# One-hots of the destinations made stationary in the attribute sums, the first layer's own share moved into the build, and another order at the build's end

## The chip, the core and the metric

The kernel is one program on one core of a Trainium2 chip. The metric is device microseconds of one execution. Five engines of the core run their own instruction streams and meet at semaphores: PE (TensorE, matrix products into the eight PSUM banks), DVE (VectorE), ACT (ScalarE), POOL (GpSimd) and SP (SyncE, which here only starts DMAs).

## The reference

Five message-passing layers on 3125 nodes and 53125 edges, then a mixture of experts. Only the graph part matters here.

```python
norm = dinv[row] * dinv[col]
h = x                                          # layer norm of the input
for l in range(5):
    edge_fea = concat([edge_attr[:, 3:] @ ew1[l], edge_attr[:, 0:3] @ ew2[l]])
    msg = norm[:, None] * (h[row] + edge_fea)
    agg = segment_sum(msg, col, num_segments=n)
    h = relu(concat([h, agg], axis=1) @ mlp_w[l] + mlp_b[l])
    h = (h - mean(h)) * rsqrt(var(h) + eps) * bn_g[l] + bn_b[l]
    if l != 4: h = relu(h)
```

The product with `mlp_w` splits in two: `h @ mlp_w[:256]`, the nodes' **own share**, and `agg @ mlp_w[256:]`. The own share of layer 0 needs nothing of the edges. The edge attributes reach `agg` only through the sum of each destination's four scaled attributes, the **attribute sums**; these are the same in all layers.

## The kernel before

All features are kept transposed: `hT` and `aggT` have 128 partitions (channels of one half h of two) and 3125 columns (nodes). The columns go in NQ = 7 groups `COLS`, six of 500 and one of 125.

**The build.** The adjacency matrix is made on the chip as counts, 25 source tiles of 125 rows by 3125 destinations (`at`). The edges, sorted by destination, are taken in 63 windows w of 50 destinations; with these inputs each window is one turn of 8 chunks of 128 edges. For a turn DVE makes three one-hot tiles (L1575 to L1582: `ohS` of the source's place, `ohD` of the destination, `cnt1`), double-buffered by `side` = w % 2, and raises `s_oh`. PE then does 8 matmuls for the attribute sums (L1817: `now`, 12 columns of attribute parts, is the stationary operand and `ohD`, 50 columns, moves) and 8 for the counts (L1819). Two windows make a pair u. After a pair PE closes the bank (L1823, `s_cnt`), ACT copies it (L1671, `s_enc`), DVE splits it in nibbles (L1545, L1549, `s_nib`) and ACT writes five pieces of `at` with sums (L1689, `s_at`). DVE does the nibbles of pair u after the window 2u + 3.

Between the windows PE has more work, in the order of its program: two transposes a window of the input's tiles (`across`, L1736; four banks, ACT copies each to `hT` at L1644 in `turned`), and **dense units**. A unit is one source tile of one group g = (column group, half): two matmuls of up to 500 columns with `m` stationary (L699). Layer 0's aggregation is 14 groups g of 25 units, 350 units in all. `dense_after(w)` says how many are done by window w: at most six a window, from window 13 on, and 50 in each ten windows, so that one window in ten (w = 22, 32, ...) has none. A group ends with its attributes (L705, which wait for `s_s4Te`), and DVE evicts it (L724).

**The attribute sums' way.** The sums of a block b of ten windows stand as 12 rows by 500 columns in bank 2 or 3. ACT copies them out (`sums_out`, L1659), PE transposes them by four tiles of 125 (`turn_sums`, L1772, in window 10b + 12), DVE adds and splits them in three bf16 parts (`attribute_sums`, L1561 to L1565), PE turns these back into rows (`turn_rows`, L1778), ACT writes them to `s4T` (`rows_out`, L1664).

**The build's end.** After window 62 PE has 100 units left (groups 10 to 13). Its order: `turn_sums(5)` in the loop, `turn_rows(5)`, 25 units, `turn_sums(6)`, 25 units, `turn_rows(6)`, a check sum, the last 50 units of 125 columns. DVE's order: the nibbles of pairs 30 and 31 (the latter wait for ACT), then both `attribute_sums`, then the evictions of groups 8 on. A group g >= 3 starts only when group g - 3 is evicted.

**The linear step** (`linear_pe`, L786): for each column group PE multiplies `wcur` with `hT` (own share) and with `aggT`, in f32, 16 matmul records a group, 8 of them own share. ACT adds the bias and takes the relu from PSUM (L886); DVE takes statistics (L846), at the end their aggregate (L849). The same code serves all layers. After it PE runs 14 matmuls on zeros (L746) until the next layer's transposes (L680).

Of the kernel before, what the change touches and what calls it, by code (L numbers as in the profile page):

```python
# [82 lines left out]
def gnn_ffn_program(nc, x, src, dst, edge_attr, mlp_w, mlp_b, ew1, ew2, bn_g, bn_b,  # L83
                    wg, bg, gbias, w1, b1, w2, b2, out):
    ctx = ExitStack()
    with ctx:
# [46 lines left out]
        r.at = max(r.at, w_at + 12288)  # L133
# [10 lines left out]
        eps = r("eps", [128, 1], F32)  # L144
# [20 lines left out]
        s4r = r("s4r", [12, CQ], F32)  # L165
# [21 lines left out]
        s4h = r("s4h", [P, BT, PARTS, PARTS, 4], BF16)  # L187
        assert r.at <= w_end
        cnt1 = []
# [138 lines left out]
        s4P = r("s4P", [P, BT, 4], F32)  # L328
# [54 lines left out]
        s_s4r = sem("s_s4r")  # L383
        s_s4t = sem("s_s4t")
# [21 lines left out]
        s_hd = sem("s_hd")  # L406
        s_ls = sem("s_ls")
# [73 lines left out]
        EWB = bank[7]  # L481

        def sums_of(b):

            return bank[2 + b % 2][0:12, 0:min(CQ, NW * W - CQ * b)]

        def tiles_of(b):

            return range(BT * b, min(BT * (b + 1), NT))
# [287 lines left out]
        def linear_pe(pe, base, following):  # L777
            pe.wait_ge(s_wc, base(1) + 1)
            for q, (a, w) in enumerate(COLS):
                pe.wait_ge(s_agge, base(H * NQ) + H * (q + 1))  # L780
                if q >= 2:
                    pe.wait_ge(s_z, base(ZC) + H * (q - 1))
                for k in range(2 * H):
                    rhs = (hT if k < H else aggT)[:, k % H, a:a + w]
                    for h in range(H):
                        last = pe.matmul(bank[2 * (q % 2) + h][:, 0:w], wcur[:, k, h * 128:(h + 1) * 128], rhs, start=k == 0, stop=k == 2 * H - 1)  # L786
                        if k == 2 * H - 1:
                            last.then_inc(s_mlp, 1)
# [22 lines left out]
        def statistics_dve(dve, base, following):  # L811
# [10 lines left out]
            if not last_layer:  # L822
# [12 lines left out]
                attribute_parts(dve, step, lambda: dve.tensor_tensor(ewS[:, :, :], ewT[:, :, :], cfi[:, 1, :].bitcast(F32).unsqueeze(2).to_broadcast([128, H, 4]), ALU.mult))  # L835
            for q, (a, w) in enumerate(COLS):
                if q == NQ - 1:
                    dve.wait_ge(s_mlp, base(H * NQ) + H * NQ)
                    step(dve.tensor_scalar(hT[:, 1, a:a + w], bank[2 * (q % 2) + 1][:, 0:w], prm[:, 0, 1:2], 0.0, ALU.add, ALU.max))
# [42 lines left out]
        def linear_act(act, base, following):  # L882
            for q, (a, w) in enumerate(COLS):
                for h in range(H if q < NQ - 1 else 1):
                    act.wait_ge(s_mlp, base(H * NQ) + H * q + h + 1)
                    act.activation(hT[:, h, a:a + w], bank[2 * (q % 2) + h][:, 0:w], ACT.Relu, bias=prm[:, 0, h:h + 1]).then_inc(s_z, 1)  # L886
# [359 lines left out]
        def _(sp):  # L1246
# [35 lines left out]

            sp.wait_ge(s_cnt, PAIRS)
# [53 lines left out]
        def _(dve):  # L1337
# [213 lines left out]
            def attribute_sums(b):  # L1551

                tiles = tiles_of(b)
                n = len(tiles)
                x, parts = s4P[:, 0:n, :], s4h[:, 0:n, :, :, :]

                def thrice(v):
                    return v.unsqueeze(2).to_broadcast([P, n, PARTS, 4])

                dve.wait_ge(s_s4t, b + 1)  # L1560
                step(dve.tensor_reduce(x, TURN[0:P, 0:12 * n].rearrange("p (t k j) -> p t j k", t=n, k=3), axis=XYZ, op=ALU.add))  # L1561
# [50 lines left out]
            with dve.If(gathers == 0):  # L1612
                for l in range(L):
                    if l:
                        aggregate_dve(dve, layer(l), LOADS * (l + 1))
                    statistics_dve(dve, layer(l), layer(l + 1) if l + 1 < L else None)
            with dve.If(gathers == 1):
                gather_dve(dve, 0)
                statistics_dve(dve, layer(0), layer(1))
# [9 lines left out]
        def _(act):  # L1629
# [12 lines left out]
            def turned(t):  # L1642
                act.wait_ge(s_xT, t + 1)
                act.activation(hT[:, :, t * P:(t + 1) * P], bank[4 + t % 4][:, 0:H * P].rearrange("p (h n) -> p h n", h=H), ACT.Copy).then_inc(s_xTe, 1)  # L1644
# [9 lines left out]

            def sums_out(b):
# [229 lines left out]
```

## Time and profile before

| | us |
|---|---|
| Median of three runs | 1605.82 (1603.84 to 1607.27) |
| The profiled execution | 1611.95 |
| its span, first to last instruction | 1610.3 |
| PE busy | 1421.4 |
| DVE busy | 674.2 |
| ACT busy | 399.4 |

The profile's page gives busy time of the engines and the chain of work that ended last. The timeline gives start and duration in microseconds; a line "x8" is eight instructions from the start of the first to the end of the last. A square bracket at its end is idle time of that engine ahead of it and who ended it. Matmul records overlap, so that the spacing of two starts, not the duration of one, is what a matmul costs in a stream. PEclk is the granted clock of TensorE, where 1.00 is 2.4 GHz and 0.50 is 1.2 GHz.

### The profile page before, as it was taken

What the parts mean: (1) busy time and instruction counts of PE and PEld (TensorE: products, weight loads), DVE (VectorE), ACT (ScalarE), POOL (GpSimd) and SP (SyncE); (2) the same over time, 40 slices, a digit from 0 to 9 for tenths busy, and PEclk for the clock granted to TensorE, in tenths of its full rate; (3) what the DMA queues carried; (4) which work ended last, traced back from release to release, by engine and by line L of the source; (5) the groups of instructions that cost most, each with busy time, mean ns of one, the idle gap of its engine ahead of it and who ended that gap; (6) DMA issues with size and microseconds to landing.
All of it is one profiled execution on the core that took longest, in us unless ns stands there. A gap on an engine that the chain in (4) does not pass through costs nothing.

```text
span 1610.3 us, 25262 instructions
## 1 busy us (share of the span) xinstructions
PE 1421.4 (88%) x9032; PEld 851.9 (53%) x9033; DVE 674.2 (42%) x1562; ACT 399.4 (25%) x1032; POOL 175.5 (11%) x147
## 2 busy tenths in 40 slices
PE   2566589999899999999999999999999873899996
PEld 2555344444444544545445554445445442899995
DVE  7989888887622310122101320023100267333442
ACT  1320354444402400033001420014100240244442
POOL 2000000000000000000000000000000003477774
PEclk9876789999989999999999999999999976999998
DMA  5144000000000000000000000000001383244443
GB/s 124 56 157 161 1 1 2 1 2 1 15 1 0 14 0 1 1 14 0 1 0 1 14 1 0 1 0 15 0 1 46 62 276 96 42 70 69 71 71 44
DMA packets 49545, 57.76 MB, mean 36 GB/s; under 512 B 14320, under 2 KB 41602, under 8 KB 49185
## 3 DMA queue, kind: packets, MB, share of 16 engines
q1 hardware_dynamic: 38688, 41.67, 9.0%
q0 software_dynamic: 10752, 14.69, 5.5%
q8 instruction: 67, 1.10, 0.3%
q14 instruction: 38, 0.30, 0.1%
HBM read 42.36 MB, written 13.99 MB: 35 GB/s over the span
## 4 chain that ended last, share of the span: by engine, by line
PE 80%; DVE 12%; issue 4%; DVEq 2%; ACT 1%; DMA 1%; POOL 1%; SPq 0%; POOLq 0%
PE bank L690 33%; PE bank L786 13%; PE bank L699 10%; PE bank L1214 6%; PE bank L1223 6%; PE bank L1819 3%; DVE ohL L1467 1%; PE bank L680 1%; PE bank L1760 1%; PE bank L705 1%; PE bank L1817 1%; PE bank L1205 1%; PE bank L1180 1%; DVEq L512 1%; PE bank L1742 1%
## 5 line engine op out<-in xcount | busy, mean ns | idle before, releaser
L690 PE MATMUL bank<-at,m 125*128 125x500 fp8e4 (+1 forms) x2800 | 550.9, 351 | 3.5 <-DVE m L647 3.5
L690 PEld LDWEIGHTS bank<-at,m 125*128 125x128 f16 x2800 | 252.4, 97 | 259.8 <-issue 7.1
L724 DVE TENSOR_TENSOR aggT<-bank,dinvB 128x500 f32<-128x500 f32 (+1 forms) x70 | 42.3, 622 | 389.0 <-PE bank L690 355.8
L886 ACT ACTIVATE hT<-bank,prm 128x500 f32<-128x500 f32 (+1 forms) x65 | 42.5, 654 | 569.2 <-PE bank L786 569.2
L699 PE MATMUL bank<-at,m 125*128 125x500 fp8e4 (+1 forms) x700 | 155.4, 376 | 6.8 <-issue 2.5
L935 POOL TENSOR_TENSOR idJ<-idJ,wts 125x1400 f32<-125x1400 f32 x2 | 8.0, 4006 | 1346.0 <-DVE idJ L1093 1346.0
L1214 PEld LDWEIGHTS bank<-xtT,w1c 128*128 128x128 f32 x896 | 111.2, 196 | 2.8
L1214 PE MATMUL bank<-xtT,w1c 128*128 128x128 f32 x896 | 111.4, 279 | 0.0
L786 PE MATMUL bank<-hT,wcur 128*128 128x500 f32 (+1 forms) x280 | 111.1, 539 | 0.0
L786 PE MATMUL bank<-aggT,wcur 128*128 128x500 f32 (+1 forms) x280 | 110.8, 538 | 0.0
L699 PEld LDWEIGHTS bank<-at,m 125*128 125x128 f16 x700 | 63.5, 103 | 83.6 <-issue 33.5
L1223 PE MATMUL bank<-w2s,h1T 128*128 x448 | 106.1, 380 | 0.0
L846 DVE BATCH_NORM_STATS2 zst<-hT 128x6 f32<-128x500 f32 x60 | 40.9, 681 | 153.2 <-ACT hT L886 153.2
L647 DVE SCALAR_TENSOR_TENSOR m<-bank,dinvP,m 125x256 f16<-125x256 f32 x100 | 47.3, 483 | 132.6 <-ACT m L669 132.6
L951 POOL DMA_INDIRECT out_rows<-ytb,rowS x56 | 95.7, 1709 | 53.1 <-issue 23.5
L1689 ACT ACTIVATE at<-encB 125x500 fp8e4<-125x500 uint8 (+1 forms) x96 | 57.5, 599 | 120.7 <-DVE encB L1545 118.1
L1223 PEld LDWEIGHTS bank<-w2s,h1T 128*128 128x128 f32 x448 | 80.8, 190 | 9.2 <-issue 0.2
L786 PEld LDWEIGHTS bank<-aggT,wcur 128*128 128x128 f32 x280 | 50.4, 190 | 55.1 <-issue 55.1
L786 PEld LDWEIGHTS bank<-hT,wcur 128*128 128x128 f32 x280 | 50.1, 190 | 53.4 <-issue 53.2
L1580 DVE TENSOR_TENSOR cnt<-iotaK,nowKD 128x2000 bf16<-128x2000 int16 x63 | 75.2, 1194 | 0.0
L1819 PE MATMUL bank<-cnt,ohS 128*128 128x250 bf16 x504 | 74.3, 293 | 0.0
L1000 ACT ACTIVATE h1T<-bank,b1T 128x128 f32<-128x128 f32 x224 | 64.0, 368 | 25.4 <-issue 20.5
(318 smaller groups left out, 1413.8 us busy)
## 6 DMA issues: line engine op xcount, KB each, us to landing
slrow<-sl_dram SPq DMA_DIRECT2D x26, 512.0 KB, 4.8
w1s<-in_L_ffn_W SPq DMA_DIRECT2D x1, 4096.0 KB, 13.8
w2s<-in_L_ffn_W SPq DMA_DIRECT2D x1, 4096.0 KB, 20.5
xin<-in_x SPq DMA_DIRECT2D x1, 2800.0 KB
x<-in_x SPq DMA_DIRECT2D x1, 2800.0 KB
out_rows<-x SPq DMA_DIRECT2D x1, 2800.0 KB
xn_dram<-xn SPq DMA_DIRECT2D x1, 2800.0 KB
wraw<-in_L_gnn_mlp_w SPq DMA_DIRECT2D x5, 512.0 KB, 3.5
```

The source lines that it names most:

```text
L647: dve.scalar_tensor_tensor(m[:, t, 1, :], bank[t % 4][0:P, 0:D], dinvP[:, t:t + 1], m[:, t, 0, :], ALU.mult, ALU.subtract).then_inc(s_lo, 1)
L690: last = pe.matmul(bank[LATER[g % len(LATER)]][:, 0:w], m[:, s, k, h * 128:(h + 1) * 128], at_block(g // H)[:, s, :], start=False, stop=s ...
L699: pe.matmul(bank[FIRST[g % len(FIRST)]][:, 0:w], m[:, s, k, h * 128:(h + 1) * 128], at_block(g // H)[:, s, :], start=s == 0 and k == 0, st ...
L786: last = pe.matmul(bank[2 * (q % 2) + h][:, 0:w], wcur[:, k, h * 128:(h + 1) * 128], rhs, start=k == 0, stop=k == 2 * H - 1)
L886: act.activation(hT[:, h, a:a + w], bank[2 * (q % 2) + h][:, 0:w], ACT.Relu, bias=prm[:, 0, h:h + 1]).then_inc(s_z, 1)
L951: pool.indirect_dma_start(out[:, :], bass.IndirectOffsetOnAxis(ap=rowS[:, j:j + 1], axis=0), ytb[:, j % XB, :], None, compute_op=ALU.add). ...
L1000: last = act.activation(h1T[:, u, k, :], bank[4 + u][:, k * TT:(k + 1) * TT], ACT.Relu, bias=b1T[:, bass.ds(e, 1), k:k + 1].rearrange("p a ...
L1214: last = pe.matmul(bank[4 + u][:, k * TT:(k + 1) * TT], w1c[:, u, h, k * 128:(k + 1) * 128], xtT[:, u, h, :], start=h == 0, stop=h == H - 1)
L1223: last = pe.matmul(bank[6 + u][:, 0:D], h1T[:, u, k, :], w2s[:, bass.ds(e, 1), k, :].rearrange("p a f -> p (a f)"), start=k == 0, stop=k = ...
L1580: dve.tensor_tensor(cnt1[side][:, :, :, :], to_all(iotaK[:, :, :], U // 2), by_pairs(nowKD[:, side, 0, :], GW), ALU.is_equal)
L1689: last = act.activation(at_block(q)[:, field:field + FIELDS * (GROUPS - 1) + 1:FIELDS, a:a + n], byte[:, f, :, 0:n], ACT.Copy, saturate=False,
L1819: last = pe.matmul(out_w, ohS[side][:, j // 2, :, j % 2], cnt1[side][:, j // 2, :, j % 2].rearrange("p (g n) -> p g n", g=GROUPS), start=F ...
```

## The change

Three things. In the attribute sums the operands change places: `ohD` is stationary (50 columns) and `now` moves (12 columns). The sums of a window stand as 50 rows by 12 columns, so that DVE reads them from PSUM without `sums_out` and `turn_sums`; `turn_rows` works with ten strips of 50 rows in place of four tiles of 125.

The own share of layer 0 is computed in the build: PE does it for column group q after window 2q + 4 (`own_share`), ACT adds the bias and writes it back into `hT`; the weights come by a DMA of their own (`w1z`). In layer 0 PE then does only the `aggT` half; DVE adds the own share (`add_own`), ACT takes the relu. Since the own share takes banks 6 and 7, `across` has two banks in place of four.

At the build's end PE takes six units before `turn_rows(5)` and 44 behind it; DVE takes `attribute_sums(5)` and the evictions of groups 8 and 9 before the nibbles of pair 31; ACT writes the rows of block 5 before its last pieces of `at`.

```diff
@@ attribute_sums (DVE)
-                dve.wait_ge(s_s4t, b + 1)
-                step(dve.tensor_reduce(x, TURN[0:P, 0:12 * n].rearrange(...), axis=XYZ, op=ALU.add))
+                dve.wait_ge(s_s4, b + 1)
+                if b:
+                    dve.wait_ge(s_s4T, b)
+                step(dve.tensor_reduce(x, sums_of(b).rearrange("p (t k j) -> p t j k", t=n, k=3), axis=XYZ, op=ALU.add))
@@ the build's end (DVE)
-            for u in range(PAIRS - 2, PAIRS):
-                low_nibbles(u)
-                high_nibbles(u)
+            low_nibbles(PAIRS - 2)
+            high_nibbles(PAIRS - 2)
             attribute_sums(NQ - 2)
+            dve.wait_ge(s_cnt, PAIRS)
+            for g in range(evicted, H * NQ - 2 * H):
+                evict(dve, zero, g, FIRST)
+            low_nibbles(PAIRS - 1)
+            high_nibbles(PAIRS - 1)
             attribute_sums(NQ - 1)
...
-            for g in range(evicted, H * NQ - H):
+            for g in range(H * NQ - 2 * H, H * NQ - H):
@@ statistics (DVE)
+            def add_own(q):
+                a, w = COLS[q]
+                for h in range(H):
+                    dve.wait_ge(s_mlp, H * q + h + 1)
+                    dve.tensor_tensor(hT[:, h, a:a + w], bank[2 * (q % 2) + h][:, 0:w], hT[:, h, a:a + w], ALU.add).then_inc(s_ad, 1)
+            if first_layer:
+                add_own(0)
             for q, (a, w) in enumerate(COLS):
+                if first_layer and q + 1 < NQ:
+                    add_own(q + 1)
@@ SP
+            sp.wait_ge(s_ds, NLB)
+            sp.dma_start(w1z[:, :, :], mlp_w[0:1, 0:D, :].rearrange("a (k p) c -> p (a k) c", p=128)).then_inc(s_wz, 16)
+                sp.dma_start(biasz[:, :], mlp_b[0:1, :].rearrange("a (h p) -> p (a h)", p=128)).then_inc(s_wz, 16)
@@ the pairs (ACT)
-                        sums_out(b)
                 for t in range(4 * u + (u > 0), min(4 * u + 5, NT)):
                     turned(t)
+                if 2 <= u < NQ + 2:
+                    a, w = COLS[u - 2]
+                    act.wait_ge(s_pz, u - 1)
+                    for h in range(H):
+                        act.activation(hT[:, h, a:a + w], OWN[h][:, 0:w], ACT.Identity, scale=2.0 ** -H0_EXP, bias=biasz[:, h:h + 1]).then_inc(s_hz, 1)
+                if u == PAIRS - 1:
+                    rows_out(NQ - 2)
@@ PE
             def across(t):
-                if t >= 4:
-                    pe.wait_ge(s_xTe, t - 3)
+                if t >= 2:
+                    pe.wait_ge(s_xTe, t - 1)
+            def own_share(q):
+                a, w = COLS[q]
+                pe.wait_ge(s_xTe, min((q + 1) * BT, NT))
+                if q == 0:
+                    pe.wait_ge(s_wz, 32)
+                    pe.wait_ge(s_ewm, 1)
+                else:
+                    pe.wait_ge(s_hz, H * q)
+                for k in range(H):
+                    for h in range(H):
+                        last = pe.matmul(OWN[h][:, 0:w], w1z[:, k, h * 128:(h + 1) * 128], hT[:, k, a:a + w], start=k == 0, stop=k == H - 1)
+                last.then_inc(s_pz, 1)
+                        if g == 1:
+                            pe.wait_ge(s_hz, H * NQ)
-                        pe.matmul(sums_w, now[:, side, 0:12, j], ohD[side][:, j // 2, :, j % 2], start=False, stop=False)
+                        pe.matmul(sums_w, ohD[side][:, j // 2, :, j % 2], now[:, side, 0:12, j], start=False, stop=False)
-                for t in range(2 * w + (w > 0), min(2 * w + 3, NT)):
+                for t in range(2 * w + (w > 1), min(2 * w + 2 + (w > 0), NT)):
                     across(t)
-                if w > SB and w % SB == 2:
-                    turn_sums(w // SB - 1)
+                if w >= 4 and w % 2 == 0 and w // 2 - 2 < NQ:
+                    own_share(w // 2 - 2)
+            done = dense_to(min(done + DENSE_W, DENSE))
             turn_rows(NQ - 2)
-            done = dense_to(min(done + NT, DENSE))
-            turn_sums(NQ - 1)
-            done = dense_to(min(done + NT, DENSE))
+            done = dense_to(min(done + 2 * NT - DENSE_W, DENSE))
             turn_rows(NQ - 1)
```

## Rows read from the trace of the kernel before

**Rows 1.** Timeline, PE in windows 3 and 4: start, us, engine, line, form, idle before.
```profile
180.73 0.36 PE L1817 MATMUL bank<-ohD,now 128*12 128x50 bf16 x8 [1.22 <-DVE ohS L1582]
...
181.94 0.16 PE L1823 MATMUL bank<-zeros 128*128 128x1 bf16 x1
...
182.82 0.38 PE L1808 MATMUL bank<-zeros 128*128 128x500 bf16 x1
...
184.67 0.36 PE L1817 MATMUL bank<-ohD,now 128*12 128x50 bf16 x8 [1.47 <-DVE ohS L1582]
```

**Rows 2.** Timeline, PE: turns of windows 13, 14, 15 and 23, window 14's units.
```profile
218.65 0.49 PE L1817 MATMUL bank<-ohD,now 128*12 128x50 bf16 x8 [1.15 <-DVE ohS L1582]
...
225.59 0.39 PE L1817 MATMUL bank<-ohD,now 128*12 128x50 bf16 x8
...
227.11 2.71 PE L699 MATMUL bank<-at,m 125*128 125x500 fp8e4 x12
...
229.75 0.39 PE L1817 MATMUL bank<-ohD,now 128*12 128x50 bf16 x8
...
263.10 0.49 PE L1817 MATMUL bank<-ohD,now 128*12 128x50 bf16 x8 [1.21 <-DVE ohS L1582]
```

**Rows 3.** Timeline, PE from the last window to the last units.
```profile
438.55 0.60 PE L1772 MATMUL bank<-ident,s4r 12*125 12x12 f32 x4
...
444.35 0.60 PE L1778 MATMUL bank<-negI,s4h 125*36 125x125 bf16 x4 [5.20 <-DVE s4h L1565]
444.88 13.29 PE L699 MATMUL bank<-at,m 125*128 125x500 fp8e4 x50
...
460.86 12.14 PE L699 MATMUL bank<-at,m 125*128 125x500 fp8e4 x50 [2.17 <-DVE aggT L724]
```

**Rows 4.** Table by stretch, linear step: us, busy time (instructions) of each engine, PEclk, DMA.
```profile
480.00:500.00 20.00, 20.00 (x49) 9.03 (x48) 5.52 (x22) 3.39 (x5) 0.00 (x0) 1.00 0.00 1
```

**Rows 5.** Timeline, layer 0's linear step: own shares of groups 0 and 5, end, next layer.
```profile
479.65 3.62 PE L786 MATMUL bank<-hT,wcur 128*128 128x500 f32 x8
...
513.29 3.52 PE L786 MATMUL bank<-hT,wcur 128*128 128x500 f32 x8
...
523.35 0.55 DVE L849 BATCH_NORM_AGGREGATE zmv<-zst 128x2 f32<-128x42 f32 x2
...
526.80 0.67 PE L680 MATMUL bank<-ident,hT 128*125 128x128 f32 x4 [0.60 <-DVE hT L644]
```

**Rows 6.** Timeline, window 1: the bank's close, ACT's copies, the transposes behind them.
```profile
175.09 0.16 PE L1823 MATMUL bank<-zeros 128*128 128x1 bf16 x1
175.32 0.59 ACT L1671 ACTIVATE encI<-bank 125x500 int32<-125x500 f32 x1 [21.18 <-PE bank L1823]
...
175.81 1.46 ACT L1644 ACTIVATE hT<-bank 128x250 f32<-128x250 f32 x5
...
176.24 0.43 PE L1736 MATMUL bank<-ident,xin 125*128 125x125 f32 x2 [0.34 <-ACT hT L1644]
```

**Rows 7.** The page's groups: busy us, mean ns, idle before and its releaser.
```profile
L724 DVE TENSOR_TENSOR aggT<-bank,dinvB 128x500 f32<-128x500 f32 (+1 forms) x70 | 42.3, 622 | 389.0 <-PE bank L690 355.8
...
L846 DVE BATCH_NORM_STATS2 zst<-hT 128x6 f32<-128x500 f32 x60 | 40.9, 681 | 153.2 <-ACT hT L886 153.2
...
L1689 ACT ACTIVATE at<-encB 125x500 fp8e4<-125x500 uint8 (+1 forms) x96 | 57.5, 599 | 120.7 <-DVE encB L1545 118.1
```

**Rows 8.** Instructions by line: ns min/median/max, first and last start, forms (PEld: weight loads).
```profile
L1817 PE MATMUL bank<-ohD,now x504: 183/186/220, 170.4 to 437.3; 128*12 128x50 bf16 x168
...
L1825 PEld LDWEIGHTS bank<-zeros x7: 84/84/84, 204.7 to 438.5; 128*12 128x12 bf16 x7
...
L1778 PEld LDWEIGHTS bank<-negI,s4h x25: 93/98/155, 231.3 to 473.2; 125*36 125x36 bf16 x25
...
L1772 PEld LDWEIGHTS bank<-ident,s4r x25: 178/183/184, 216.9 to 458.4; 12*125 12x125 f32 x25
```

**Rows 9.** Timeline, the lookups ahead of the build: 25 columns moving, 128 stationary.
```profile
150.65 1.36 PE L1760 MATMUL bank<-dpart,ohT 125*128 125x25 bf16 x48
```

More of the change, by code:

```diff
@@ L781, in linear_pe @@
                 if q >= 2:
-                    pe.wait_ge(s_z, base(ZC) + H * (q - 1))
-                for k in range(2 * H):
+                    pe.wait_ge(s_ad, H * (q - 1)) if first else pe.wait_ge(s_z, base(ZC) + H * (q - 1))
+                for k in range(first, 2 * H):
                     rhs = (hT if k < H else aggT)[:, k % H, a:a + w]
                     for h in range(H):
-                        last = pe.matmul(bank[2 * (q % 2) + h][:, 0:w], wcur[:, k, h * 128:(h + 1) * 128], rhs, start=k == 0, stop=k == 2 * H - 1)
+                        last = pe.matmul(bank[2 * (q % 2) + h][:, 0:w], wcur[:, k, h * 128:(h + 1) * 128], rhs, start=k == first, stop=k == 2 * H - 1)
                         if k == 2 * H - 1:
@@ L1692, in _ @@
                 last.then_inc(s_at, 1)
-            for b in range(NQ - 2, NQ):
-                rows_out(b)
+            rows_out(NQ - 1)
             for l in range(L):
@@ L1766, in _, with turn_rows @@
             pe.wait_ge(s_xn, NT)
-            def turn_sums(b):
-                pe.wait_ge(s_s4r, b + 1)
+            def own_share(q):
[4 more added lines that the diff above has]
+                    pe.wait_ge(s_ewm, 1)
+                else:
+                    pe.wait_ge(s_hz, H * q)
[3 more added lines that the diff above has]
+                last.then_inc(s_pz, 1)
+            def turn_rows(b):
                 pe.wait_ge(s_s4Te, b) if b else pe.wait_ge(s_xTe, NT)
-                for n, t in enumerate(tiles_of(b)):
-                    last = pe.transpose(TURN[0:P, 12 * n:12 * (n + 1)], s4r[:, n * P:(n + 1) * P], ident[0:12, 0:12])
-                last.then_inc(s_s4t, 1)
-            def turn_rows(b):
                 pe.wait_ge(s_s4K, b + 1)
-                for n, t in enumerate(tiles_of(b)):
-                    last = pe.matmul(TURN[0:K4, n * P:(n + 1) * P], s4h[:, n, :, :, :].rearrange("p a b j -> p (a b j)"), negI[0:P, 0:P], start=True, stop=True)
+                for n in range(strips_of(b)):
+                    last = pe.matmul(TURN[0:K4, n * W:(n + 1) * W], s4h[:, n, :, :, :].rearrange("p a b j -> p (a b j)"), negI[0:W, 0:W], start=True, stop=True)
                 last.then_inc(s_s4T, 1)
@@ L1810, in _ @@
                     if b >= 2:
-                        pe.wait_ge(s_s4r, b - 1)
-                    pe.matmul(sums_of(b), zeros[:, 0:12], nought(sums_of(b).shape[1]), start=True, stop=False)
+                        pe.wait_ge(s_s4K, b - 1)
+                    pe.matmul(sums_of(b), zeros[:, 0:W], nought(12 * strips_of(b)), start=True, stop=False)
                 with pe.Fori(0, mine) as i:
```

80 lines of the change are left out of this document (41 added, 39 removed).

## The prediction

> **What bounds the kernel now.** The page's busy times come first: PE works 1421 of 1610 us, so a change pays where PE waits, runs at half clock or loses work. The timeline of PE then shows four stretches that the change touches. In the early windows PE waits for DVE's one-hots: 1.22 us ahead of window 3, 1.47 ahead of window 4 [rows 1]. From window 13 on six dense units fill a window and PE is the bound: windows 14 and 15 start without a wait, 4.16 us apart [rows 2]. Window 13 itself lasts 6.94 us (218.65 to 225.59): its eight sums take 0.49 us where window 14's take 0.39, which is TensorE at 1.2 GHz in place of 2.4 after the waits before it [rows 2]. One window in ten has no units; there PE waits 1.21 us for DVE and falls to half clock again (window 23, 0.49) [rows 2]. At the build's end PE stands 5.20 us for the split of block 5's sums, and 2.17 us for an eviction [rows 3]. In layer 0's linear step PE is busy without a hole at granted clock 1.00 [rows 4]; a column group takes (513.29 - 479.65) / 5 = 6.73 us, and its own share half of it, 3.36 [rows 5].
>
> **The linear step of layer 0.** Six own shares of 500 columns leave it: 6 x 3.36 = 20.2 us off the path. The seventh, of 125 columns (about 0.9, a quarter), goes into the tail. DVE takes on two adds a group, of the eviction's form (PSUM and SBUF in, 0.62 us), beside two statistics of 0.68 [rows 7]: 2.6 us in 3.36, so PE stays the bound, though narrowly. ACT's relu, now from SBUF, hangs behind the add, not in PE's way. What is late next is the tail. Today group 5 ends at 479.65 + 6 x 6.73 = 520.0, and the aggregate of the statistics starts at 523.35, 3.3 us on [rows 5]. Afterwards DVE has, from the end of group 5, one add 0.62, group 4's statistics 1.36, two adds of 125 columns 0.6 (taken at half), group 5's statistics 1.36, a relu 0.3, two small statistics 0.7, and some 0.3 of gaps: 5.2. So the step gains 20.2 - 1.9 = **18.3 us**. Bounds: 20 if the tail hides, 15 if DVE's 2.6 became more than PE's 3.36 by a tenth or two.
>
> **The start of layer 1.** PE's idle time ahead of the next transposes is 0.60 us today [rows 5], because the 14 matmuls on zeros end just before them. PE now finishes some 1.9 us earlier against DVE, so it stands about 2.5 us. A hole of 2.17 us was followed by a slowed stretch [rows 3], priced below at 1.3. I take **+1 us**, between 0 and the 2.8 that window 13 lost.
>
> **The build's end.** A 500-column matmul in a clean stream costs (2.71 - 0.38) / 11 = 0.212 us (twelve in 2.71 [rows 2]; one record of 500 columns lasts 0.38 [rows 1]), so 50 of them 49 x 0.212 + 0.38 = 10.8. Group 10 took 13.29 and group 11 12.14 [rows 3]: 2.5 and 1.3 us of half clock behind the two holes. With six units first, `turn_rows(5)` comes 2.7 us after the last window. Its input, DVE's `attribute_sums(5)`, then waits only for the nibbles of pair 30, not for those of 31, so it is done before. Group 11 needs group 8's eviction, which DVE does at once after window 62. ACT writes block 5's rows while PE is in group 10, before it is asked for them. Behind each of the two steps that DVE moves ahead stand the nibbles of pair 31, which wait for ACT's copy anyway and are needed only 10 us later, by group 12. The gain is 5.20 + 2.17 + 2.5 + 1.3 + 0.6 (`turn_sums(5)`, four transposes [rows 3]) = 11.8, with the single transpose of block 6 **12 us**. Bounds: 4 if the first hole stays, 12.5.
>
> **The own share in the build.** PE gets 6 x 3.36 + 0.9 = 21 us more, in windows 4 to 16. What of it is hidden? The windows 4 to 13 take (218.65 - 184.67) / 4.5 = 7.55 us a pair [rows 1, 2]. After: the odd window has its turn, 1.21 (180.73 to 181.94 [rows 1]). Its transposes now have two banks and wait for ACT's copy of a tile, which stands behind the copy of the counts: 1.15 us from the bank's close to the transposes (175.09 to 176.24 [rows 6]), where 0.4 stands today. Two transposes with a copy of 0.29 (1.46 / 5 [rows 6]) between them take 0.8, the zeros for the next pair 0.3: 3.5 in all. The even window: turn 1.21, two transposes 0.65 (0.88 from the close to the zeros, less the dispatch [rows 1]), the share 3.36: 5.2. A pair takes 8.7, so +1.2, over 4.5 pairs +5.4, and +1 once in window 3, where ACT still writes pair 0's pieces when PE asks for a tile. Then share 5 in window 14 adds its 3.4, share 6 in window 16 0.9, and group 1 waits perhaps 0.5 in window 17 until ACT has emptied bank 6. Against that, PE is busy before window 13, so its 6.94 become 4.16: -2.8, since f32 matmuls hold clock 1.00 [rows 4]. Sum **+8.5 us**. Bounds: +1.5 if the five early shares fit wholly into the waits (3.4 + 0.9 - 2.8), +21 if nothing is hidden. ACT has room for the 14 new copies (about 0.6 each, 1.3 a pair): it sat 118 us waiting for nibbles over 32 pairs, 3.7 a pair [rows 7]. On SP the two new DMAs follow the lookups and are landed long before window 4; nothing queued behind them is wanted before the last window.
>
> **The sums with the one-hots stationary.** Today eight matmuls span 0.36 us and one lasts 0.186 [rows 1, 8]: (0.36 - 0.186) / 7 = 25 ns each, with 50 columns moving. The lookups, with 25 columns moving and 128 stationary, run at (1.36 - 0.19) / 47 = 25 ns too, one record taken as long [rows 9]. So 12 columns save nothing; a gain is excluded as far as that row reaches. A cost could come from loading 50 columns where 12 were. Loads of bf16 take 84 ns for 12 columns and 93 at the least for 36, 0.38 ns a column; the f32 load of 125 columns takes 183 [rows 8], 0.88 a column above the first. At 0.38, 50 columns are 19 ns and hide within the 25. At 0.88 they are 44, 19 more a matmul, 0.15 a turn, over some 45 turns where PE is the bound 6.8 us. I take the bf16 rows, of the same type and shape: **0**, bounds 0 and +7. The Trainium skill speaks against this change: TensorE: Matmul & The Clock Gate, section LDWEIGHTS (loading the stationary operand), gives a load's time as its columns divided by 1.2 (ns), and section Weight-path perf modes makes only full loads of 128 fast. By that, 50 columns are 42 ns and the sum is 6 us worse; the two bf16 rows here grow at less than half of that rate.
> The removed turns sit in the window in ten in which PE waits 1.21 us for DVE [rows 2], so they give nothing but at the end (counted). DVE's split now handles 120 elements on 50 partitions in place of 48 on 125, perhaps +0.4 us a block. It stands in the window where PE is at half clock behind DVE, so 0; without that cover 6 x 0.4 = 2.4.
>
> **Sum.** +8.5 + 0 - 12 - 18.3 + 1 = -20.8. The profiled execution took 1611.95 (span 1610.3 and 1.65 around it), which becomes 1591.2. That execution stands 6.1 above the median of the runs, so the median becomes 1605.82 - 20.8 = 1585.0.
>
> **The rivals.**
> Loads bind the sums: 50 stationary columns at 0.88 ns each, +6.8, **1592**. For it: the 125-column row and its slope. Against: the bf16 rows. This is also what the skill's rule would give, within a microsecond.
> The early shares hide wholly: +1.5 in place of +8.5, **1578**. For it: PE's waits of 1.2 to 1.5 us in each early window [rows 1]. Against: the wait for ACT between the two transposes.
> A hole stays at the end: `attribute_sums(5)` still stands behind the nibbles of pair 30, which need ACT's copy after pair 29's pieces; were those late, PE would stand again and fall to half clock. 5.2 + 2.5 given back, **1593**.
> Slower than before: TensorE stays at 1.2 GHz in windows 4 to 17, because short f32 bursts between waits don't lift it. A share then takes 6.7, all seven 42, no wait is long enough to hide them, and window 13 gains nothing. 42 - 12 - 18.3 + 1 = +12.7, **1618**. It decides from a build cost of 29 us on. For it: window 13's half clock after windows of short work. Against: the granted 1.00 of the same matmuls in the linear step, and the fuller windows.
> The build cost lands between, near 14 to 16 (two waits a pair in place of one): **1591**.
>
> **How the numbers follow.** Forecast 0.46 (1585, own range 1581 to 1589); loads 0.16; cost between 0.11; hidden wholly 0.11; hole 0.08; half clock 0.04, and 0.04 for a build that just eats the gain. 0.2% is 3.2 us, about what the runs here can tell apart. All cases but the last two are below 1602: faster 0.92, same 0.03, slower 0.05. The range reaches from the wholly hidden case to two of the costs together: 1577 to 1598.
>
> **What would show it.** Right: the distance from window 3 to 13 grows by 5 to 7 us and window 13 takes about 4.2; the eight sums still 0.36 to 0.39; no PE hole over 1 us between window 62 and the linear step, and that stretch near 29 us; the linear step from 43.7 to about 25 us, with DVE's adds ending inside PE's groups. Wrong: eight sums at 0.45 or more (loads), shares of 6.7 (clock), a wait at L1778 after window 62 (hole), or DVE adds well above 0.62, which would make DVE the bound of the step.

## The result, and the profile of the changed kernel

| | before | after |
|---|---|---|
| Median | 1605.81 (1603.84 to 1607.27, six runs) | 1588.11 (1586.53 to 1593.09, six runs) |
| Ratio | | 0.9896, 95% interval 0.9879 to 0.9912 |
| Profiled execution | 1611.95 | 1591.14 |
| its span | 1610.3 | 1589.4 |

The changed kernel is 17.7 us faster; 20.8 were forecast. To see where, both spans are cut at the same points of the program: the starts of the counts of windows 3, 13 and 62, of the linear step's first matmul, of the statistics' aggregate and of the 13th record of layer 1's transposes. Both kernels were later profiled once more, unchanged ("again"); those columns become important below.

| stretch, us | before | after | before again | after again |
|---|---|---|---|---|
| start to window 3 | 181.0 | 182.7 | 181.3 | 181.3 |
| windows 3 to 13 | 38.1 | 43.4 | 38.1 | 43.4 |
| windows 13 to 62 | 218.4 | 218.8 | 213.5 | 217.8 |
| window 62 to the linear step | 42.2 | 30.0 | 40.2 | 30.0 |
| linear step to the aggregate | 43.7 | 24.7 | 43.7 | 24.7 |
| aggregate to layer 1's 13th transpose | 12.6 | 15.6 | 12.6 | 14.3 |
| the rest | 1074.3 | 1074.1 | 1074.7 | 1073.9 |

**Early windows.** Timeline of PE in the changed kernel, from the close of one pair through the next (columns as in [rows 1]):

```profile
183.79 0.16 PE L1859 MATMUL bank<-zeros 128*128 128x1 bf16 x1
184.93 0.71 PE L1763 MATMUL bank<-ident,xin 125*128 125x125 f32 x4 [0.98 <-ACT hT L1676]
...
185.78 0.39 PE L1853 MATMUL bank<-now,ohD 128*50 128x12 bf16 x8
...
187.80 3.52 PE L1805 MATMUL bank<-hT,w1z 128*128 128x500 f32 x8
191.25 0.39 PE L1853 MATMUL bank<-now,ohD 128*50 128x12 bf16 x8
...
194.48 0.39 PE L1853 MATMUL bank<-now,ohD 128*50 128x12 bf16 x8
```

The wait for one-hots [rows 1] is gone, but PE stands 0.98 us ahead of an odd window's transposes. With two banks they wait until ACT has copied a tile that the even window transposed, and ACT copies the pair's counts first. The share takes 3.5 us at full clock. The next such waits end at 193.63 and 202.41, so a pair takes 8.7 to 8.8 us, where it took 7.55.

**The end.** Timeline of PE from the last window's turn; it answers to [rows 3]:

```profile
446.08 2.71 PE L704 MATMUL bank<-at,m 125*128 125x500 fp8e4 x12
448.72 0.42 PE L1812 MATMUL bank<-negI,s4h 50*36 50x50 bf16 x10
449.07 8.21 PE L704 MATMUL bank<-at,m 125*128 125x500 fp8e4 x38
...
457.53 10.75 PE L704 MATMUL bank<-at,m 125*128 125x500 fp8e4 x50
...
474.95 20.39 PE L791 MATMUL bank<-aggT,wcur 128*128 128x500 f32 x48
```

There is no hole of PE up to the linear step. Group 10 takes 2.71 + 8.21 and group 11 10.75, where they took 13.29 and 12.14 behind holes of 5.20 and 2.17.

**The linear step.** Timeline of DVE in it; the bracket is DVE's idle time and who ended it:

```profile
484.48 0.68 DVE L845 TENSOR_TENSOR hT<-bank,hT 128x500 f32<-128x500 f32 x1 [0.67 <-PE bank L791]
485.31 0.68 DVE L845 TENSOR_TENSOR hT<-bank,hT 128x500 f32<-128x500 f32 x1 [0.16 <-PE bank L791]
485.91 1.25 DVE L865 BATCH_NORM_STATS2 zst<-hT 128x6 f32<-128x500 f32 x2
...
499.69 0.55 DVE L868 BATCH_NORM_AGGREGATE zmv<-zst 128x2 f32<-128x42 f32 x2
```

DVE waits for PE in each group (0.67 + 0.16 us of 3.36), so PE is still the bound. [rows 5]'s aggregate came 43.7 us after the step's start; now it comes 24.7 after.

**The start of layer 1.** Timeline of PE ahead of and behind the next transposes:

```profile
497.98 3.16 PE L751 MATMUL bank<-zeros 128*128 128x500 bf16 x14
503.14 0.67 PE L685 MATMUL bank<-ident,hT 128*125 128x128 f32 x4 [2.00 <-DVE hT L649]
504.68 3.52 PE L695 MATMUL bank<-at,m 125*128 125x500 fp8e4 x8 [0.87 <-DVE m L652]
```

The matmuls on zeros now end 2.00 us before they are relieved (0.60 in [rows 5]), and the eight matmuls behind take 3.52 us; at full clock they take 1.86 (below).

### The profile page after: what moved, and what is told of

It is laid out like the page before. It is cut to its first block, busy times and chain, and to the rows that moved or that the text cites. A ratio compares the mean times of both kernels' runs of the same rounds, so it can differ in the third digit from the quotient of the medians.

```text
span 1589.4 us, 25320 instructions
## 1 busy us (share of the span) xinstructions
PE 1408.4 (89%) x9045; PEld 846.1 (53%) x9046; DVE 681.6 (43%) x1576; ACT 403.7 (25%) x1039; POOL 174.9 (11%) x147
## 4 chain that ended last, share of the span: by engine, by line
PE 81%; DVE 11%; issue 3%; ACT 1%; DVEq 1%; DMA 1%; POOL 1%; SPq 0%; POOLq 0%
PE bank L695 34%; PE bank L791 12%; PE bank L704 9%; PE bank L1237 6%; PE bank L1246 6%; PE bank L1855 3%; PE bank L1787 2%; DVE ohL L1494 2%; PE bank L685 1%; PE bank L1805 1%; PE bank L1853 1%; PE bank L710 1%; PE bank L1228 1%; PE bank L1203 1%; PE bank L1181 1%
## 5 line engine op out<-in xcount | busy, mean ns | idle before, releaser
L909 ACT ACTIVATE hT<-bank,prm 128x500 f32<-128x500 f32 (+1 forms) x52 | 34.0, 654 | 529.5 <-PE bank L791 529.5
L865 DVE BATCH_NORM_STATS2 zst<-hT 128x6 f32<-128x500 f32 x60 | 40.2, 679 | 123.6 <-ACT hT L909 123.6
L791 PE MATMUL bank<-hT,wcur 128*128 128x500 f32 (+1 forms) x224 | 88.8, 539 | 0.0
L674 ACT ACTIVATE m<-bank,dinvP 125x256 f16<-125x256 f32 x100 | 46.1, 473 | 98.0 <-PE bank L685 97.2
## 6 DMA issues: line engine op xcount, KB each, us to landing
w2s<-in_L_ffn_W SPq DMA_DIRECT2D x1, 4096.0 KB, 20.9
```

Source lines behind the costliest of these rows:

```text
L674: act.activation(m[:, t, 0, :], bank[t % 4][0:P, 0:D], ACT.Copy, scale=dinvP[:, t:t + 1]).then_inc(s_hi, 1)
```

## The experiments

**Both kernels once more, unchanged.** In the first profile of before, the five windows that follow a window without units or an idle stretch (13, 23, 33, 43, 53) lasted 6.8 us each from counts to counts, mostly at 1.2 GHz (granted clock 0.56).

> The kernel before, unchanged, profiled once more. In the profile that the prediction rests on, windows 13, 23, 33, 43 and 53 each run wholly at half clock (6.8 us from turn to turn), while three changed kernels show 5.5 to 6.3 there. Theory (how far the clock falls in those windows differs from execution to execution, and the first profile caught a long one, 6 us above the median): here these windows last 5.4 to 6.3 us, window 62 starts 3 to 6 us earlier than 437.1, and the time is 1603 to 1608. Rival (the kernel before always falls that far, the turned sums cure it): 6.8 us again, and the profile's surplus lies elsewhere.

> The changed kernel, unchanged, on the chip of the other runs of this call: the base for them. Both theories: 1586 to 1591 and a ratio of 0.987 to 0.991.

Measured: before 1605.83 us, span 1604.1; after 1589.10 (1587.13 to 1591.10), ratio 0.9894 [0.9878, 0.9911], span 1585.4. The five windows of before now take 5.50, 6.02, 6.39, 5.45 and 5.71 us. Timeline of PE in window 23 of that profile; [rows 2] has it in the other:

```profile
262.04 0.37 PE L1817 MATMUL bank<-ohD,now 128*12 128x50 bf16 x8 [1.21 <-DVE ohS L1582]
...
263.68 4.22 PE L699 MATMUL bank<-at,m 125*128 125x500 fp8e4 x12 [0.26 <-issue]
```

Behind the same wait of 1.21 us the eight sums take 0.37 us here and 0.49 there, and only the units are slow, 4.22 in place of 2.71. So the clock falls later, or for less time, behind the same idle stretch: how much it costs differs from execution to execution. The first profile had the expensive end of it, all five times, and was 6.2 us longer. Between the two second profiles the change is -18.7 us: build to window 62 +9.6, end -10.2, linear step -18.95, start of layer 1 +1.7, the rest -0.8. Between the two first ones it is -20.9: +7.5, -12.2, -18.95, +3.0, -0.2.

**One part at a time.** The theory is that the three parts add, with the prices of the prediction.

Sums alone, with the split and `turn_rows` that go with them and without `sums_out` and `turn_sums`; own share and order of the end as before.

```diff
-                        pe.matmul(sums_w, now[:, side, 0:12, j], ohD[side][:, j // 2, :, j % 2], start=False, stop=False)
+                        pe.matmul(sums_w, ohD[side][:, j // 2, :, j % 2], now[:, side, 0:12, j], start=False, stop=False)
...
```

> Only the turned attribute sums: own share in the linear step and the old order at the end. Theory (a stream of 8 small matmuls runs at 25 to 27 ns each in both forms, and the removed turns stood beside a wait for DVE): within 2 us of the kernel before, 1604 to 1607, window 62 within 1 us of 437.1. Rival A (loads of 50 columns bind): 6 us slower than before. Rival B (the removed turns and copies are worth something in every ten windows): 3 to 6 us faster than before.

Measured: 1604.39 us, ratio 0.9996 [0.9986, 1.0006]. From window 22 to 62 it takes 173.9 us, before again 174.1: operands in either place cost the same. At the end PE stands 5.98 us for the split, but the 2.17 us wait for an eviction is gone: 37.8 us from window 62 to the linear step against 40.2.

Sums and order, own share left in the linear step, `across` with its four banks again:

```diff
-                if w >= 4 and w % 2 == 0 and w // 2 - 2 < NQ:
-                    own_share(w // 2 - 2)
...
-                    linear_pe(pe, layer(l), layer(l + 1) if l + 1 < L else None, 0 if l else H)
+                    linear_pe(pe, layer(l), layer(l + 1) if l + 1 < L else None)
...
```

> The changed kernel with the own share back in layer 0's linear step (16 records a group, no add on DVE, transposes on four banks as before). Theory: window 62 starts 7.5 us earlier, at about 437; the linear step is 19 us longer; layer 1 starts at full clock again, 3 us gained: 8.5 us slower than the changed kernel, about 1596 to 1597. Rival (the 7.5 us of the build are due to the turned sums, as slower weight loads would make them): window 62 stays at 443 or later and the kernel is 16 us slower, 1604.

Measured: 1596.55 us (1594.75 to 1598.52), ratio 0.9952 [0.9935, 0.9968]. The linear step begins 30.0 us after window 62, 7.8 earlier than with the sums alone, and the two medians differ by 7.8: that is the order's worth. Window 62 comes at 432.8 us, where before again has 432.9 and after again 442.5; so the whole +9.7 in the build is the own share, with the two banks that it leaves to `across`. Against it stand -18.95 in the linear step and +1.7 behind it: -7.5 in the traces, and 7 to 9 less in the runs (1589.10 against 1596.55, of two chips; 0.9894 against 0.9952 of before).

The changed kernel with the old order at its end, on DVE and ACT too:

```diff
-            done = dense_to(min(done + DENSE_W, DENSE))
             turn_rows(NQ - 2)
-            done = dense_to(min(done + 2 * NT - DENSE_W, DENSE))
+            done = dense_to(min(done + NT, DENSE))
+            done = dense_to(min(done + NT, DENSE))
             turn_rows(NQ - 1)
...
```

> The changed kernel with the old order at the build's end (PE: turn_rows(5) ahead of the units; DVE: both nibbles, both attribute_sums, then the evictions; ACT: rows of block 5 last). Theory (each part gives what the sum of steps says): the holes of 5.2 and 2.2 us and the half clock behind them come back, 12 us lost against the changed kernel (1588 to about 1600); everything up to window 62 stays. Rival (the holes belong to the old sums' way and are mostly gone with turn_sums, or the later end of the windows has let ACT and DVE catch up): 3 to 6 us lost, a hole of under 3 us at turn_rows(5).

Measured: 1598.73 us (1593.14 to 1602.10), ratio 0.9956 [0.9939, 0.9973]. Timeline of PE behind the last window:

```profile
454.57 0.57 PE L1807 MATMUL bank<-negI,s4h 50*36 50x50 bf16 x10 [5.98 <-DVE s4h L1593]
455.07 13.14 PE L704 MATMUL bank<-at,m 125*128 125x500 fp8e4 x50
...
468.45 10.75 PE L704 MATMUL bank<-at,m 125*128 125x500 fp8e4 x50
```

The hole is back, and behind it group 10 loses 13.14 - 10.75 = 2.4 us at half clock: 8.4 us together, of the 10 by which the medians differ. Put in last, the order is thus worth some 10 us, and put on top of the sums alone 7.8; this kernel's runs spread over 9 us, so the parts add within what can be told apart. The wait for an eviction doesn't come back. It was missing with the sums alone too, so the order didn't remove it. Timeline of DVE at the end of the kernel before:

```profile
458.72 0.17 DVE L1561 TENSOR_REDUCE s4P<-bank 125x4 f32<-125x12 f32 x1 [14.43 <-PE bank L1772]
...
460.05 1.84 DVE L724 TENSOR_TENSOR aggT<-bank,dinvB 128x500 f32<-128x500 f32 x3
```

DVE stood 14.43 us for `turn_sums(6)`, which PE did behind group 10, and evicted only after it. Without `turn_sums(6)` its last split no longer waits for PE's group 10.

**Does the load of the stationary operand bind the sums?** `ohS`, which has 128 columns to take from, stands in for `ohD`, so that the attribute sums are left out of the result; the window number modulo 3 sets 50, 100 or 124 columns.

```diff
+                wide = (50, 100, 124)[w % 3]
...
-                        pe.matmul(sums_w, ohD[side][:, j // 2, :, j % 2], now[:, side, 0:12, j], start=False, stop=False)
+                        pe.matmul(bank[2 + b % 2][0:wide, 12 * (w % SB):12 * (w % SB + 1)], ohS[side][:, j // 2, 0:wide, j % 2], now[:, side, 0:12, j], start=False, stop=False)
```

> Measures the cost of a stationary load by its width. In the changed kernel the sums' matmuls take the first 50, 100 or 124 columns of ohS as stationary (window w mod 3 = 0, 1, 2) with the same 12 columns moving; the attribute sums are thus left out of the result. Theory (a bf16 load costs 0.38 to 0.42 ns a column at 2.4 GHz and hides under 25 ns): spacing 26 to 28 ns at 50 columns, about 42 at 100, 52 at 124. Rival (a load costs its columns divided by 1.2 in ns unless it is a full one of 128): 42, 83 and 103 ns. Third (width does not matter for bf16): 25 to 28 at all widths.

Measured: 1582.3 us, in one run. The groups of PE by form (us busy, mean ns of one), then three turns of the timeline:

```profile
L1854 PE MATMUL bank<-now,ohS 128*124 128x12 bf16 x168 | 13.3, 209 | 4.3 <-DVE ohS L1610 4.3
L1854 PE MATMUL bank<-now,ohS 128*100 128x12 bf16 x168 | 11.5, 198 | 2.5 <-DVE ohS L1610 2.5
L1854 PE MATMUL bank<-now,ohS 128*50 128x12 bf16 x168 | 8.4, 185 | 16.9 <-DVE ohS L1610 16.9
```
```profile
244.41 0.60 PE L1854 MATMUL bank<-now,ohS 128*124 128x12 bf16 x8
...
249.66 0.39 PE L1854 MATMUL bank<-now,ohS 128*50 128x12 bf16 x8
...
253.73 0.52 PE L1854 MATMUL bank<-now,ohS 128*100 128x12 bf16 x8
```

The spacing of two matmuls is (0.60 - 0.209) / 7 = 56 ns with 124 columns, (0.52 - 0.198) / 7 = 46 with 100 and (0.39 - 0.185) / 7 = 29 with 50. With 100 and 124 columns the load does set the pace, at about 0.45 ns a column; 50 columns would be 23 ns by that and hide, as the prediction took it from [rows 8]. By the rule of the Trainium skill (TensorE: Matmul & The Clock Gate, section LDWEIGHTS (loading the stationary operand)) the estimates are 42, 83 and 103 ns; the measurement decides against it for these bf16 loads. But this one run was 6 us below the changed kernel's median, though its loads are longer. That was foreseen by no theory, and led to the next two runs.

**Why are wider operands faster?** In the changed kernel the units start late behind a turn with 50 columns and its counts; with 100 they don't. The next kernel has 100 columns in every window, `ohD` and the 50 columns that lie next to it; the upper 50 rows of the products are read by nobody.

```diff
+                wide = 2 * W
...
-                        pe.matmul(sums_w, ohD[side][:, j // 2, :, j % 2], now[:, side, 0:12, j], start=False, stop=False)
+                        pe.matmul(sums_w, ohD[side][:, j // 2:j // 2 + 2, :, :].rearrange("p a w k -> p (a w) k")[:, 0:wide, j % 2], now[:, side, 0:12, j], start=False, stop=False)
```

> The changed kernel with 100 stationary columns in the attribute sums in place of 50 (the access runs on into the next chunk pair's one-hots; the 50 extra rows of the sums are not read). The load becomes longer (46 in place of 28 ns a matmul, 0.14 us a turn). In the run with mixed widths, turns with 100 or 124 columns were nevertheless 0.3 us shorter: no gap of 0.1 us ahead of the sums, none ahead of the counts, and no idle time ahead of the dense units. Theory (narrow stationary operands put the array into another tiling, and each change of it makes PE drain): turn to dense units 1.3 us in place of 1.6, DVE's work (about 42 us in ten windows) becomes the bound, windows 22 to 62 take 167 to 170 us in place of 175, the kernel is about 8 us faster than the changed one, 1580. Rival (the longer loads are what counts): 0.14 x 45 = 6 us slower, 1594.

Measured: 1574.35 us (1573.69 to 1575.59), ratio 0.9800 [0.9783, 0.9816]: 14.7 faster than the changed kernel on the same chip (1589.10), not only 8. Timeline of PE, one window of the changed kernel, then one with 100 columns:

```profile
297.99 0.39 PE L1853 MATMUL bank<-now,ohD 128*50 128x12 bf16 x8
298.32 1.08 PE L1855 MATMUL bank<-cnt,ohS 128*128 128x250 bf16 x8
299.62 0.59 PE L704 MATMUL bank<-at,m 125*128 125x500 fp8e4 x2 [0.23 <-issue]
```
```profile
292.34 0.52 PE L1856 MATMUL bank<-now,ohD 128*100 128x12 bf16 x8
292.71 1.06 PE L1858 MATMUL bank<-cnt,ohS 128*128 128x250 bf16 x8
293.61 2.70 PE L704 MATMUL bank<-at,m 125*128 125x500 fp8e4 x12
```

From the first sum to the first unit it is 1.63 us against 1.27. The medians, over the windows from 13 on at full clock in which units follow the counts directly, are 1.55 us (18 windows) and 1.27 (18 windows). The kernel before has 1.53 (20 windows): with 12 stationary columns it paid the same. Over 49 windows, 13 to 62, the gain is 217.8 - 203.6 = 14.2 us, 0.29 a window.

Is it the width as such, or a threshold? In the kernel with 100 columns the window number modulo 3 now sets 32, 64 or 72; the windows with 32 leave the sums of 18 of their 50 destinations out. The edit is shown against the kernel with 100.

```diff
-                wide = 2 * W
+                wide = (32, 64, 72)[w % 3]
```

> The changed kernel, with the one-hot's stationary operand made 32, 64 or 72 columns wide (window number modulo 3) in place of 50; the columns beyond 50 are products that nobody reads. From the first of a window's eight sums to its first dense unit it takes 1.63 us with 50 columns and 1.28 to 1.35 with 100 or 124. Theory: TensorE takes a stationary operand of up to 64 columns as another arrangement of its array, so the change between it and the 128 columns of the counts and units costs time, whatever the loads last: 32 and 64 columns give about 1.6 us, 72 about 1.3. Rival: the cost falls smoothly with the width: 32 gives about 1.7, 64 about 1.55, 72 about 1.5. The total lies between the changed kernel and the one with 100 columns, 1581 to 1588 us.

Measured: 1582.36 us in one run. Timeline of PE, sums and first units with 32, 64 and 72 columns:

```profile
276.09 0.37 PE L1856 MATMUL bank<-now,ohD 128*32 128x12 bf16 x8
...
277.82 2.71 PE L704 MATMUL bank<-at,m 125*128 125x500 fp8e4 x12 [0.35 <-issue]
...
285.30 0.43 PE L1856 MATMUL bank<-now,ohD 128*72 128x12 bf16 x8
285.58 1.06 PE L1858 MATMUL bank<-cnt,ohS 128*128 128x250 bf16 x8
286.49 2.70 PE L704 MATMUL bank<-at,m 125*128 125x500 fp8e4 x12
...
294.10 0.43 PE L1856 MATMUL bank<-now,ohD 128*64 128x12 bf16 x8
294.46 1.08 PE L1858 MATMUL bank<-cnt,ohS 128*128 128x250 bf16 x8
295.64 2.71 PE L704 MATMUL bank<-at,m 125*128 125x500 fp8e4 x12
```

From the first sum to the first unit it is 1.73 us with 32 columns, 1.19 with 72 and 1.54 with 64 in these rows; the medians are 1.56 (32 columns, 7 windows), 1.57 (64, 5 windows) and 1.22 (72, 6 windows). The step lies between 64 and 72, so it is a threshold and no smooth price of width. Nor is it the pace of the sums: with a mean duration of 0.186 us their spacing is (0.43 - 0.186) / 7 = 35 ns at 64 and at 72. This fits what the Trainium skill says (TensorEngine Tiling (Array Packing), section Key Properties): changing the tiling mode drains TensorE. That a narrow operand alone is such a change, and that a drain is what costs the time, is argued and not shown; measured is the step, 0.28 us a turn between 50 and 100 columns and 0.35 between 64 and 72. One part of it is direct: with 64 columns the counts start 0.36 us after the sums, with 72 only 0.28. The larger part lies behind the counts, as time in which PE's instructions had not been issued; what makes it was not tested.

**The hole ahead of layer 1.** Nine more matmuls on zeros there.

```diff
-            for n in range(WARM):
+            for n in range(warm):
...
-                        aggregate_pe(pe, layer(l), layer(l - 1))
+                        aggregate_pe(pe, layer(l), layer(l - 1), WARM + (9 if l == 1 else 0))
```

> The changed kernel with 9 more matmuls on zeros after layer 0's linear step (23 in place of 14, 1.9 us), so that PE has no idle time of 2.0 us ahead of layer 1's transposes. Theory (TensorE falls to 1.2 GHz there, which makes the start of layer 1 3.0 us longer than in the kernel before): from the first transposes to the seventh pair 9.2 us as before in place of 12.2, 3 us faster than the changed kernel. Rival (the 3 us are something else, or the pace there is set by ACT and DVE): no change, or up to 1 us slower.

Measured: 1589.02 us (1586.95 to 1590.28), ratio 0.9885 [0.9869, 0.9902], the same as the changed kernel beside it (1589.10). Timeline of PE in it, and below it in the kernel of the next run, which has no added zeros:

```profile
500.02 5.08 PE L751 MATMUL bank<-zeros 128*128 128x500 bf16 x23
505.18 0.67 PE L685 MATMUL bank<-ident,hT 128*125 128x128 f32 x4
506.72 1.86 PE L695 MATMUL bank<-at,m 125*128 125x500 fp8e4 x8 [0.87 <-DVE m L652]
```
```profile
496.71 0.67 PE L685 MATMUL bank<-ident,hT 128*125 128x128 f32 x4 [2.01 <-DVE hT L649]
498.25 1.86 PE L695 MATMUL bank<-at,m 125*128 125x500 fp8e4 x8 [0.87 <-DVE m L652]
```

With the idle time filled, the stretch from the first of these transposes to the 13th takes 9.2 us, as forecast. But with the same 2.0 us of idle time it took 12.2 in the first profile of after, 10.9 in the second and 9.2 in the last rows. The hole costs 0 to 3 us, by execution; filling it gains too little for these runs to show. This trace shows something else that differs by execution. Timeline of PE behind window 3:

```profile
183.73 1.09 PE L1763 MATMUL bank<-ident,xin 125*128 125x125 f32 x4 [2.93 <-ACT hT L1676]
...
188.12 4.42 PE L1805 MATMUL bank<-hT,w1z 128*128 128x500 f32 x8
```

ACT still writes pair 0's pieces when PE asks for a tile, PE stands 2.93 us in place of 0.98, and the first share runs partly at half clock (4.42 us in place of 3.52). Windows 3 to 13 take 47.7 us here and, with the same wait, 47.4 in the kernel with the old end, where the two profiles of the changed kernel have 43.4.

**Can the early wait be covered?** The share goes into the odd window before, ahead of its two transposes; ACT takes it one pair earlier.

```diff
+                if w >= 3 and w % 2 and (w - 3) // 2 < NQ:
+                    own_share((w - 3) // 2)
                 for t in range(2 * w + (w > 1), min(2 * w + 2 + (w > 0), NT)):
                     across(t)
-                if w >= 4 and w % 2 == 0 and w // 2 - 2 < NQ:
-                    own_share(w // 2 - 2)
...
```

> The changed kernel, with each column group's own share put into the odd window before it, ahead of that window's two transposes, in place of the even window after them. Theory: the build is longer because PE stands about 0.98 us in each odd early window for ACT's copy of the first transposed tile; with 3.4 us of share between, that wait is covered. Window 3 to 13 then takes some 39 us in place of 43.5, and the kernel about 1584.5 us. Rival: the early windows are set by the work itself or by DVE's and ACT's chain, and the wait only moves to another place: window 3 to 13 stays at 43 us and the time at 1588 to 1589.

Measured: 1584.89 us (1581.77 to 1587.70), ratio 0.9869 [0.9847, 0.9892]. Two of its four runs, 1587.6 and 1587.7, are as slow as the changed kernel's, so the total alone doesn't tell the theory from its rival. The profiled run is the fastest; windows 3 to 13 take 40.0 us in it in place of 43.4. Timeline of PE:

```profile
182.84 3.59 PE L1805 MATMUL bank<-hT,w1z 128*128 128x500 f32 x8 [0.38 <-issue]
186.27 0.59 PE L1763 MATMUL bank<-ident,xin 125*128 125x125 f32 x4
```

The transposes follow without the wait of 0.98 us. In this trace the theory holds: of the 5.3 us that the shares cost in these windows, 3.4 were the waits that their place left standing.

**Five units in each window**, in place of six in nine and none in the tenth.

```diff
-DENSE_W = 6
+DENSE_W = 5
```

> The changed kernel, with five dense units in each window in place of six in nine windows and none in the tenth. Theory: the window without units costs twice, by the 1 to 2 us that PE stands for DVE and by the half clock behind it (that window lasts 5.5 to 6.8 us in the runs seen); with five units a window PE keeps the clock, ten windows take about 42 us in place of 43.5, and the kernel loses about 6 us, to 1582.5. Rival: DVE, busy 145 of 174 us there, becomes the bound, PE stands a little in every window and ten windows stay at 43 to 44 us: 1588 to 1590.

> The changed kernel with 100 stationary columns (alone 1574.35 us), the shares in the odd windows, five units a window and nine more matmuls on zeros ahead of layer 1. Theory: the four add, since each takes away a wait or a hole at another place: 1574.35 - 4 - 6 - 2 = about 1562 us. Rival: with windows this short DVE bounds the build (145 us busy of 164 from window 22 to 62), so five units bring nothing more, and the warming nothing: 1570 us.

Measured for five units alone: 1579.56 us (1577.87 to 1582.16), ratio 0.9834 [0.9814, 0.9854], 9.5 us less than the changed kernel where 6 were expected. Table by stretch, windows 22 to 62 (us, then busy time of PE, PEld, DVE, ACT, POOL, then PEclk), of after again and of five units:

```profile
268.00:442.00 174.00, 158.01 (x1136) 83.25 (x1136) 144.67 (x314) 75.16 (x224) 0.00 (x0) 0.97 0.01 2
```
```profile
268.00:432.00 164.00, 153.72 (x1135) 81.50 (x1134) 144.53 (x316) 74.00 (x224) 0.00 (x0) 1.00 0.01 2
```

The stretch is 10 us shorter: 4.3 us of it is the same work at 1.00 in place of 0.97 of the clock (158.0 to 153.7 us busy), 5.7 is less standing (16.0 to 10.3). DVE's 144.5 us still fit. Five more units remain at the end, 2.5 us. All four together (100 columns, share in the odd window, five units, nine zeros): 1563.53 us (1562.78 to 1566.31), ratio 0.9733 [0.9717, 0.9750], against 1562 expected. This kernel beats both. That the expectation came out is in part luck, for the parts don't add everywhere: windows 13 to 62 are 14.2 us shorter with 100 columns alone and 12.7 with five units alone, but 19.5 in the kernel with all four.

## Why the prediction was right

**The linear step** (-18.3): -18.95 in both pairs of profiles. PE stayed the bound. DVE's add was 0.68 us where 0.62 was taken: 0.62 is the mean of a group with two forms [rows 7], and its 60 evictions of 500 columns take 0.677 each. The tail from the end of group 5, 474.95 + 6 x 3.36 = 495.1, to the aggregate is 4.6 us where 5.2 was.

**The build** (+8.5): +7.5 and +9.6 up to window 62. Most steps hold singly: a pair 8.7 forecast and 8.7 measured, though its even window takes 5.5 us of 5.2 and its odd one 3.2 of 3.5 (185.78, 191.25, 194.48); window 13 4.39 us of 4.16; window 14 with its share 7.70, 3.5 more. Windows 3 to 13 take +5.4 and +5.3, of 5.4 for the pairs and 1 for window 3. That one wait is absent in both profiles of the changed kernel; with nine more zeros and with the old end it is there, with the half clock behind it, and windows 3 to 13 take 9.6 and 9.4 us more than before. So the build's cost is known to some us only. The reason named for the pair, the wait for ACT's copy of a tile, is the one that the run with the share in the odd window took away.

**The sums** (0): shown twice, by the sums alone (0.9996) and by the spacing of 29 ns with 50 columns. The rival of binding loads falls. What the prediction did not see is that both forms pay some 0.3 us a turn for being at 64 columns or fewer. Its rows showed it, since the units of window 14 start 1.52 us after its sums [rows 2], but nothing in the profile of before had a wider operand to compare with.

**The end** (-12): -12.2 from the first pair of profiles, -10.2 from the second. The holes of 5.20 and 2.17 are gone in both. The first went as foreseen; the second would have gone without the new order too, because the turned sums had taken away what DVE waited for. The part that is mis-sized is the half clock behind them: 2.5 + 1.3 in the profile at hand; in before again group 11 takes 10.74 us, with no loss behind its wait.

**Layer 1's start** (+1, bounds 0 and 2.8): the idle time is 2.0 us (2.5 forecast), the cost 0 to 3 us by execution, +3.0 and +1.7 in the two pairs. The bounds were nearly right, and a single profile could not have fixed the size.

**The sum** came out 3 us too good, 20.8 for 17.7. From profile to profile the first pair gives just the forecast, -20.9 us, but by luck: layer 1's start cost 2.0 us more than forecast, while the build cost 1.0 less and the linear step and the end gained 0.65 and 0.2 more. The step that failed is the move from the profiled execution to the median. That execution was 6.1 us above its median, the changed kernel's profiled one 3.0 above its own, and the sum was subtracted from the median as it stood. But three of its terms, the -2.8 of window 13 and the 2.5 and 1.3 at the end, were half-clock losses read in just this long execution. In before again, which took 1605.83 us, window 13 has 5.50 us from counts to counts in place of 6.83, and the stretch at the end 40.2 in place of 42.2: some 3.4 us of the gain weren't there in an ordinary run.

No rival came true: no hole at the end, no loads that bind, no half clock in the shares beyond the first one of two other executions (3.5 us each, 4.2 and 4.4 there), and a build cost of 7.5 to 9.6 us, not hidden. A cost of 14 for two waits a pair didn't come either; where window 62 came 14 us after that of before again, at 447.0 and 447.4, it was the one wait at window 3 and the clock.

## What to carry to other kernels

Moving work off the critical path into waits pays only after its own new waits: the own share saved 19 us and cost 10 in the build, of which 3.4 were a wait in each pair that another order of the same instructions covered. Where short matmuls with a narrow stationary operand stand between full ones, pad the operand beyond 64 columns and time it: 50 useless columns here made the kernel 0.9% faster. A loss to the clock read in one profile is one draw: when that execution is above the median, put such terms into a sum as a range.

## What the runs showed of the hardware that was not expected

- A stationary operand of 12, 32, 50 or 64 columns between operands of 128 costs 0.3 us a turn more than one of 72 or 100 (1.53 to 1.57 us against 1.22 to 1.27 from the first sum to the units), though the loads of the latter are longer.
- Short matmuls with bf16 operands are spaced by the width of the stationary one: 46 ns with 100 columns and 56 with 124, about 0.45 ns a column; 35 ns with 64 and 72; with 32 and 50 it stays at 27 to 29 ns.
- The same idle time ahead of the same work cost between nothing and 3 us of half clock: at layer 1's start with 2.0 us, and in window 23 of before (6.79 and 6.02 us behind a wait of 1.21).
- With 100 columns and five units a window the gap ahead of the units is back in part: the median from first sum to units is 1.5 us in the last kernel. Between windows 22 and 62 PE stands 3.5 us ahead of units in it, 1.0 with 100 columns alone and 5.1 in after again. So the width isn't the whole of that gap; what else sets it stays open.
